# Later due times for attention and routing, and a reciprocal of 64 sums with a copy, in a decoder layer on one core

## The reference, cut to what matters

```
x = LN(x + recurrent_attention(x))     # 16 heads of 16; a 16x16 state for each head, token by token
x = LN(x + cross_attention(x, ctx))    # softmax over 77 keys, 16 heads, then @ Wo.T + bo
x = LN(x + shared_out + routed_out)    # 2 shared experts; the best 2 of 8 routed ones for each token
```

## Time and profile before

| | |
|---|---|
| median of 3 runs | 2667.95 us (2667.38 to 2668.91) |
| profiled execution | 2668.34 us, its span 2666.6 us |
| VectorE busy | 2216.5 us, 83% of the span |
| TensorE busy (matmul) | 1832.6 us, 69% |
| GpSimd, ScalarE busy | 945.9 us, 35%; 777.7 us, 29% |
| mean granted TensorE clock | 0.802 |
| chain that ended last | DVE 38%, PE 35%, ACT 10%, issue 8%, DMA 4%, POOL 3% |
| periods 0 to 4, 5, 6, 7, tail, start about | 59, 310, 600, 877, 1155, 1437, 1699, 2025, 2363 us |

### The profile page before, as it was taken

The page is one execution under the profiler, slowest core; times in us unless marked ns, Lnnn a source line. Parts: engine busy times, 40 slices in busy tenths (PEclk is TensorE's granted clock), DMA queues, the critical chain, the costliest instruction groups (busy, mean ns, idle before and its releaser), DMA issues.

```text
span 2666.6 us, 33083 instructions
## 1 busy us (share of the span) xinstructions
PE 1832.6 (69%) x9438; PEld 1383.8 (52%) x9438; DVE 2216.5 (83%) x6434; ACT 777.7 (29%) x2209; POOL 945.9 (35%) x1148
## 2 busy tenths in 40 slices
PE   3356887788768866977788831056878558876975
PEld 2234666566646755665556721034576335754664
DVE  2999959997999979997999999998998899964000
ACT  1422135312621262226321210052212521215221
POOL 5503341343234142505152546344463533220101
PEclk7557998899779978988889965566899668986998
DMA  8000331224132323242223420000145002350144
GB/s 256 11 1 12 115 129 62 99 101 149 54 119 97 123 82 112 73 149 89 78 95 124 155 73 24 8 11 1 56 147 189 27 1 86 129 192 4 55 154 138
DMA packets 175119, 238.60 MB, mean 89 GB/s; under 512 B 28657, under 2 KB 148074, under 8 KB 174954
## 3 DMA queue, kind: packets, MB, share of 16 engines
q1 hardware_dynamic: 140874, 194.46, 21.3%
q10 hardware_dynamic: 27936, 25.44, 2.9%
q0 software_dynamic: 6144, 16.79, 2.0%
HBM read 202.09 MB, written 33.16 MB: 88 GB/s over the span
## 4 chain that ended last, share of the span: by engine, by line
DVE 38%; PE 35%; ACT 10%; issue 8%; DMA 4%; POOL 3%; ACTq 1%; SPq 0%; POOLq 0%; DVEq 0%; PEldq 0%
PE ps L626 8%; PE ps L617 7%; DVE ps L1459 7%; DVE ps L1440 7%; PE ps L569 6%; DVE prod L1432 6%; ACT probs L816 5%; PE ps L562 5%; DVE terms L1447 5%; DVE terms L1442 3%; DMA pj<-in_wpT 2%; DVE rec_out L1388 1%; PE ps L479 1%; DVE rec_in L1388 1%; PE ps L465 1%
## 5 line engine op out<-in xcount | busy, mean ns | idle before, releaser
L617 PE MATMUL ps<-xg,fc 128*128 128x128 f32 x2848 | 373.9, 295 | 111.8 <-ACT vec L781 77.7
L1459 DVE TENSOR_REDUCE ps<-terms 128x64 f32<-128x320 f32 x1024 | 449.2, 485 | 0.0
L617 PEld LDWEIGHTS ps<-xg,fc 128*128 128x128 f32 x2848 | 363.3, 209 | 135.1 <-issue 126.6
L1440 DVE TENSOR_REDUCE ps<-prod 128x16 f32<-128x272 f32 x1024 | 397.7, 434 | 0.0
L1447 DVE TENSOR_TENSOR terms<-ps,rec_out 128x256 f32<-128x256 f32 x1024 | 381.7, 415 | 0.0
L1432 DVE TENSOR_TENSOR prod<-ps,rec_in 128x256 f32<-128x256 f32 x1024 | 381.1, 414 | 0.0
L626 PE MATMUL ps<-pj,hT 128*128 128x256 f32 x1424 | 335.9, 389 | 37.0 <-ACT hT L892 37.0
L626 PEld LDWEIGHTS ps<-pj,hT 128*128 128x128 f32 x1424 | 266.6, 192 | 91.3 <-ACT hT L892 57.6
L1102 POOL TENSOR_TENSOR oprod<-SE_out,rec_q 128x320 f32<-128x320 f32 x171 | 147.2, 861 | 450.4 <-DVE SE_out L1451 450.4
L562 PE MATMUL ps<-xtf,fc 128*128 128x512 f32 x512 | 253.8, 637 | 10.9 <-ACT vec L781 10.9
L569 PE MATMUL ps<-pj,hT 128*128 128x256 f32 x1024 | 236.6, 382 | 0.0
(11 more groups left out here) (200 smaller groups left out, 3004.3 us busy)
## 6 DMA issues: line engine op xcount, KB each, us to landing
fc<-in_wfcT SPq DMA_DIRECT2D x80, 1024.0 KB, 5.1
pj<-in_wpT SPq DMA_DIRECT2D x80, 1024.0 KB, 8.0
xg_rows<-in_rows ACTq DMA_DIRECT2D x105, 128.0 KB, 2.0
out_rows<-y ACTq DMA_DIRECT2D x89, 128.0 KB, 5.7
in_rows<-o_rows SPq DMA_DIRECT2D x2, 2176.0 KB, 17.8
out_rows<-o_rows SPq DMA_DIRECT2D x2, 2176.0 KB, 17.2
xtp<-in_xT SPq DMA_DIRECT2D x32, 128.0 KB, 2.4
xin<-in_x SPq DMA_DIRECT2D x8, 512.0 KB, 6.6
```

What stands on the lines that cost most here:

```text
L617: i = mm(ps[:, UP + g // 4, g % 4 * P:(g % 4 + 1) * P], fc[:, par, c, g * P:(g + 1) * P], xg[:, c], start=c == 0, stop=c == KC - 1)
L1440: red(SE[:, old, cols, HD:EH].rearrange("p v n -> p n v"), prod[:, :, cols, 0:HD + 1], AX.X, ALU.add).then_inc(step_done, 1)
L1459: red(SE[:, new, cols, 0:HD], terms[:, cols, :, 0:NV + 1], AX.X, ALU.add).then_inc(step_done, 1)
```

## The change

Three edits. (1) In `FREE_AT` everything from `minima` on moves back: `minima` from t = 24 to 34, `divisors` 44 to 53, `divided` 48 to 57, the residual sum and its norm 62 to 71, `routing` 82 to 89, `gather` 84 to 90, `scatter` 95 to 101, `combine` 104 to 108, the last norm 105 to 109. GpSimd's jobs take their places from the same table. The first norm stays at 1, and the bound table is as it was. (2) The reciprocal is taken of the 64 sums alone, into `rden`; a copy then writes each 16 times into `rden_wide`, and `spread_sums` reads that behind a new semaphore, `widened`. This holds for all eight tiles. (3) `banks_read(3)` leaves `second` and stands ahead of `router`, behind expert 9; for a bound period the same place has `banks_read(1)`.

```diff
--- before
+++ after
@@ -121,7 +121,8 @@
-        rden = sb("rden", [P, B, H, HD])
+        rden = sb("rden", [P, B, H])
+        rden_wide = sb("rden_wide", [P, B, H, HD])
@@ -503,12 +504,12 @@  spread_sums on TensorE
-                pe.wait_ge(rden_done, m + 1)
+                pe.wait_ge(widened, m + 1)
                 pe.wait_ge(acc_sb, m * 2 + 1)
                 for c in range(KC):
                     for b in range(B):
                         i = nc.tensor.transpose(ps[:, ACC + c, b * P:(b + 1) * P],
-                                                rden[:, b, c * 8:(c + 1) * 8].rearrange("p h d -> p (h d)"), ident[:, :])
+                                                rden_wide[:, b, c * 8:(c + 1) * 8].rearrange("p h d -> p (h d)"), ident[:, :])
@@ -698,10 +699,10 @@  second() and period() on TensorE
                         if m is not None:
                             pe.wait_ge(resid, m * 2 + 2)
                         prep(2)
-                        banks_read(3)
 
                 last_experts(f, (start, attend, weigh, finish, second))
                 if m is not None:
+                    banks_read(1 if bound else 3)
                     router(m)
@@ -1253,7 +1254,9 @@  divisors on VectorE
                     dve.wait_ge(exp_done, m * B + B)
-                    nc.vector.reciprocal(rden[:, :, :, :], weight_sum[:, :, :].unsqueeze(3).to_broadcast([P, B, H, HD])).then_inc(rden_done, 1)
+                    nc.vector.reciprocal(rden[:, :, :], weight_sum[:, :, :]).then_inc(rden_done, 1)
+                    dve.wait_ge(rden_done, m + 1)
+                    nc.vector.tensor_copy(rden_wide[:, :, :, :], rden[:, :, :].unsqueeze(3).to_broadcast([P, B, H, HD])).then_inc(widened, 1)
@@ -1532,7 +1535,7 @@
-FREE_AT = {1: 1, "minima": 24, "divisors": 44, "divided": 48, "resid": 62, 2: 62, "routing": 82, "gather": 84, "scatter": 95, "combine": 104, 3: 105}
+FREE_AT = {1: 1, "minima": 34, "divisors": 53, "divided": 57, "resid": 71, 2: 71, "routing": 89, "gather": 90, "scatter": 101, "combine": 108, 3: 109}
```

More of the change, by code:

```diff
@@ L208, in decoder_layer @@
          cap_half, cap_done, x1T_ps, x1T_sb, q_ps, q_sb, sc_ps, sc_sb, capped, min_done, exp_done, eT_ps,
-         eT_sb, rden_done, attT_ps, spread_ps, spread_sb, attT_sb, wo_ps, resid, x2T_ps, doubled, x2T_sb, rt_ps, rt_sb,
+         eT_sb, rden_done, widened, attT_ps, spread_ps, spread_sb, attT_sb, wo_ps, resid, x2T_ps, doubled, x2T_sb, rt_ps, rt_sb,
          route, w_done, picked, pos_ps, bounds_done, bounds_seen_pe, bounds_seen_act, gx_ps, gx_sb, xo1_ps,
@@ L216, in decoder_layer @@
             sum_seen prep_pool block_laid v_placed step_done decayed copied o_terms o_sums o_ready cap_half
-            cap_done x1T_ps x1T_sb q_ps q_sb sc_ps sc_sb capped min_done exp_done eT_ps eT_sb rden_done
+            cap_done x1T_ps x1T_sb q_ps q_sb sc_ps sc_sb capped min_done exp_done eT_ps eT_sb rden_done widened
             attT_ps spread_ps spread_sb attT_sb wo_ps resid x2T_ps doubled x2T_sb rt_ps rt_sb route w_done picked
```

## The result

The changed kernel takes 2702.57 us (median of 4 runs, 2701.77 to 2703.08) against 2667.66 (2667.08 to 2668.91, 4 runs of the kernel before on the same chip): ratio 1.013, 95% interval 1.0112 to 1.0148. It is slower by 34.9 us. Forecast were 2707 and slower; both held, the time by 4.4 us.

A forecast was written before the change was run, and what follows sets the result against it. A loop over VectorE and TensorE was taken to bound periods 1 to 4: three loops + 26.8 us, with period 0 + 13.5, the end of period 4 - 0.7 and periods 6 and 7, total + 38.8: 2707 us (2680 to 2722).

The forecast's parts named there:

- S to R: VectorE's arc from the start of `minima` to the end of the residual sum: 89.3 us, 80.5 before.
- The copy: VectorE's copy of the small reciprocal to 1024 elements: 0.65 us, hidden in the wait for the spread sums.
- The stall at the rsqrt: VectorE's norm behind the residual sum waits 11.0 us, since GpSimd's rsqrt now stands behind `k_square`.
- R to P: From the residual sum's end to the start of TensorE's `places`, which waits for `chosen`: 49.3 us, 52.0 before.
- P to S: From the start of `places` to the next start of `minima`: taken as 148 us, 145.9 before in period 2.
- Rival (b): GpSimd's rsqrt is answered at once, without the norm's stall; loop 276.8 us, total 2653 us; chance 0.06.
- TensorE's two waits: TensorE idles 9 to 10 us before the second `prepare` and about 7 us before `places`.
- rival (a): As forecast, but TensorE stays at speed across its waits: `prepare` 8.6, 146 behind `places`; 2690 us; chance 0.14.
- R to S: Arc from the residual sum's end to the next start of `minima`: 197.3 us, 197.8 before.
- Rival (d): The combine comes too early, waits 3 to 5 us for gathers, and the loop grows as much: 2720 us; chance 0.07.
- Rival (c): `minima` waits for a fixed moment, so later due times cut its wait: 2580 or about 2632 us; chance 0.03.
- (e): Rival: the gains of the banks and the lay-out offset the rest; no change, 2668 us; chance 0.04.

The follow-up runs named there:

- e4: Changed kernel with residual sum and its norm at t = 65, routing and what follows at old places: 2601.47 us, 0.9745 of the kernel before.
- e3: Changed kernel with GpSimd's second-block preparations starting at c = 5, behind the rsqrt, in free periods: 2645.58 us, 0.9908 of the kernel before.
- e1: Changed kernel with the old due times, so small reciprocal with copy and moved bank wait alone: 2657.13 us, 0.9952 of the kernel before.
- e6: Sum-at-65 kernel with the old reciprocal over 1024 elements, no copy, no `widened`: 2618.95 us, 0.9816 of the kernel before.
- e5: Sum-at-65 kernel with the bank wait back in `second`, ahead of expert 9: 2624.08 us, 0.9836 of the kernel before.
- e9: All-later kernel (e7) with routing at 89 instead of 92, gather 90, scatter 101, combine 111, last norm 112: 2610.12 us, 0.9784 of the kernel before.
- e7: Changed kernel with later due times (routing 92), a table of its own for period 0, and e3's queue order: 2599.26 us, 0.9743 of the kernel before.

## Why the prediction was right

**The loop decides, not the due time of `minima`.** Shown: ten t later took 5.1 us off period 2's wait at `minima` (15.86 to 10.76) while the loop grew by 8.5. The same ten t with the sum only three t later (e4) give a kernel 68 us faster than the one before.

**S to R, 89.3 forecast: 89.5.** The parts were as put: reciprocal 0.55 us, `divided` waiting 4.49 for the spread sums, the lay-out inside the arc. In period 1 TensorE came to the spread sums earlier, `divided` waited 2.32, and the arc was 87.2: this made that loop 283.7 and not 286.6.

**The copy: 0.65 forecast, 0.69 measured.** The Trainium skill ("VectorE: DVE Perf Modes", The perf-mode tier table) gives a float32 copy within SBUF two elements a cycle, 0.6 us here as an estimate from its table (1.1 at one a cycle); the trace agrees, also for a source of which each element is read 16 times.

**The stall at the rsqrt, 11.0 forecast: 10.34 to 10.75 in periods 0 to 3, 13.66 in period 4** (13.4 forecast there). e3 changes only where the preparations stand in GpSimd's queue, and its loop is 13.7 us shorter: 8.7 from R to P, 2.9 from P to S and 2.1 from S to R. Rival (b) had put a time on this case, 2653; measured were 2645.6. So it is shown that this order makes the changed kernel slower than the one before.

**TensorE's two waits**, 9 to 10 and about 7 us forecast: 10.20 and 7.72. `prepare` took 10.29 us (forecast 10.84), P to S 149.2 (148), its first eight matmuls 3.76 us as in the earlier trace rows. This refutes rival (a). R to P was 48.1 for 49.3. That R to S came out at 197.3, as forecast to the tenth, is luck: the two parts were off by 1.2 us each way. In period 1 TensorE waited only 2.45 us for the sum, where 9 to 10 were forecast, and `prepare` still took 9.91.

**Rival (d)** was right that the combine would wait (3.94, 4.24, 4.22, 2.26 us) and wrong that the loop would pay: with these waits the loops of periods 2 and 3 took 286.8 and 286.5 us, and the 286.6 forecast had no term for them. What paid was the slack at `minima`: one sign of being right was a wait of 12 to 14 us there, and it was 10.7 to 10.9. VectorE came some 2.5 us later to it than forecast, and the combine's 4.24 us are the one wait on its way there that the forecast had put at nothing. **Rival (c)** fell with the loops, and **(e)** with the ratio, 1.0112 at least.

**The sum.** Start of `minima` in period 1: + 12.4 (forecast 13.5). Three loops: + 23.9 (26.8). Behind period 4: - 1.7 (- 1.5). Together + 34.7 in the profiled execution for + 38.8. The mis-sized term is the loop of period 1, by 2.9; no step failed.

**What the prediction did not see** is how near a gain lay. It took the end of the bank wait as offset by `chosen`; with the queue order right the due times pay 11.6 us (e3 against e1). The reciprocal and the bank wait pay 12 us together with the old times (e1) and some 17 and 22 when they are taken out of e4 one by one (e6, e5). e4 without both was not run, so what they are worth together there is open.

## What to carry to other kernels

Where a wait comes back each period, draw the loop through all engines before moving a due time, and price both arcs. When a job moves in a hand-written order, ask what stands before it in that engine's queue and what that waits for: here two short operations behind `k_square` cost some 57 us. Slack hides edits: test each one again on the version in which the waits are gone, since two parts that were worth 12 us together may be worth 17 and 22 one by one there.

## What the runs showed of the hardware

TensorE's clock made small waits dear. A wait of 2.66 us in e9 was followed by 13 us at 0.50; 0.68 us at the same place in e7 was followed by 1.00. In e7 TensorE also idles 6.00 us ahead of the router; the clock fell to 0.50 during that wait and stood there for the 6.15 us behind it. Between short and long, length alone doesn't tell: 2.98 us in period 3 of the kernel before (at 961.70) were followed by 8 us at 1.00. TensorE's row of that wait, then the clock behind it, then behind the router's wait in e7:

```profile
961.70 0.43 PE L599 MATMUL ps<-ident,xg_rows 128*128 128x128 f32 x2 [2.98 <-ACT hT L892]
```

```profile
961.70:969.70 8.00, 5.62 (x30) 4.46 (x30) 8.00 (x23) 3.77 (x12) 2.06 (x2) 1.00 0.36 118
```

```profile
748.85:755.00 6.15, 6.15 (x21) 5.00 (x22) 6.15 (x21) 2.75 (x3) 5.55 (x7) 0.50 0.17 49
```

`prepare`, the same 28 matmuls in periods 1 to 3, took 6.91 us behind a wait of 1.03 (e4), 8.61 behind 1.38 (e6), 9.82 behind 4.09 (e6) and 10.29 behind 10.20 (changed).

The reciprocal goes by elements: 0.55 us for 64 a partition against 6.55 for 1024 (e6), so writing a result 16 times is better left to a copy (0.69).
